# ScalarE's second exponentials ahead of its first cast, statistics of x1 behind the second maximum of slot 4, gates and bias scaled by GpSimd, in a gated attention block on one Trainium2 core

## The chip, the cores and the metric

One core of a Trainium2 chip. The metric is device time in microseconds, the median of several runs of the whole program. Engines: TensorE (PE; PEld for its weight loads), VectorE (DVE), ScalarE (ACT), GpSimd (POOL), SyncE (SP, which issues most DMAs). Each engine has a queue of its own that runs in the order of the program; queues wait for each other by semaphores.

## The reference, cut to what matters

```python
# x: 8 x 256 x 128, ctx: 8 x 512 x 128, 16 heads of 64, 8 experts of capacity 160
x = x + tanh(g_xattn) * xattn(layernorm(x), ctx)   # own layernorm, q, k, v, softmax, w_out, bias b_out, times tanh(gate)
x = x + tanh(g_ffn) * moe(layernorm(x))            # 8 experts, top 1, first come first served up to 160 tokens
```

For each of 8 batches `xattn` takes softmax(q k^T / 8) v over 512 context rows, for 16 heads and 256 queries; its output is projected, gets `b_out`, and is scaled by two tanh gates. What follows is called x1. Each row of x1 is normalised (a token), its router logits choose an expert, and the token's place among that expert's tokens decides whether it is kept.

## The kernel before, in words

**Slots.** The attention is cut into 8 batches of 8 slots; a slot is one pair of heads (`hp`, 0 to 7), numbered `j` = 8 x batch + `hp`, 64 in all. The order in every queue is written out by hand: each engine has a function `batch(b)` that goes over the slots and says what the engine does in each, with step constants (`PART_STEP`, `PROJECT_STEP`, ...) for the work that comes once a batch. A slot has two halves `qt` of 128 queries.

**What happens in a slot.** *TensorE* (lines 1429 to 1467): the scores of both halves, into psAB and psCD (`scores`, lines 1247 to 1272; the second half's wait for `exp_done` of the slot before), once-a-batch transposes, the transposes of finished outputs, the projections of k and q two slots ahead into psEF, in slot 1 and 3 the output projection of the batch before, a value projection into psX, and the value matmuls of the pair two slots back (`values`, lines 1274 to 1299), which read the transposed probabilities PT; 48 matmuls, half of them for each `qt`. *VectorE* (lines 1068 to 1117): the negated row maximum of half 0 and from it the bias NB (`row_max`, lines 910 to 917), the low part of the values (`v_lo`, line 907, waits for ScalarE's `v_hi` of the slot before), once-a-batch work, the maximum of half 1, the low part of k and q (`kq_lo`), and the normalising of the head outputs of two slots back. *ScalarE* (lines 787 to 806): the exponentials of half 0 (`exps`, line 757), the high part of k and q two slots ahead (`kq_hi`; not for pairs 0, 2 and 7 of a batch, which are kept whole), the cast of half 0's probabilities to 16 bits (`phi`, line 767), the exponentials of half 1, a copy of transposed outputs (`ot_copy`), the cast of half 1, and `v_hi` (line 724). *GpSimd* (lines 629 to 668): for each half, the low part of the probabilities that the cast left over (line 660), with some work of the batch ahead of, or behind, the two. *SyncE* (lines 487 to 500): for each half a DMA that transposes high and low part into PT (line 484), behind GpSimd's low part of that half.

Each matrix product is made of high and low parts, so the probabilities need both casts and the low parts before they are transposed.

**What the change touches.** `x_rstd`, `xn`, `token_rstd` and `token` of GpSimd normalise x for the next batch and tokens of the batch before. `token_moments` (lines 961 to 973) is VectorE's statistics of x1 for the batch before, in slot 3 behind `add_attention`, `kq_lo` and `normalise_heads`; GpSimd's `token_rstd` (lines 591 to 598) and first `token` stand at the head of slot 4, the second `token` at the head of slot 5, followed by `xt_lo` (line 558). In slot 2 of batch 0 VectorE multiplies two gates into `gscale` and scales `bo` by it (lines 1112 and 1115); `bo` is used by GpSimd from slot 7 on, `gscale` by VectorE from slot 1 of batch 1. The order on ScalarE now:

```python
exps(b, hp, 0)
kq_hi(*next_pair(b, hp, AHEAD))   # not for a whole pair
phi(b, hp, 0)
exps(b, hp, 1)
ot_copy(ot_pair(j))
phi(b, hp, 1)
v_hi(*v_group(b, hp))
```

Of the kernel before, what the change touches and what calls it, by code (L numbers as in the profile page):

```python
# [26 lines left out]
ALU = mybir.AluOpType  # L27
# [6 lines left out]
def gated_block(nc, x, ctx_1024, g_xattn, g_ffn, ln_gamma, ln_beta, w_q, w_kv, w_out, b_out, gate,  # L34
# [34 lines left out]
    with ExitStack() as ctx:  # L69
# [146 lines left out]
        bo_in = sem("bo_in")  # L216
# [149 lines left out]
        PART_STEP, CTX_STEP, PROJECT_STEP = 1, 2, 3  # L366
# [45 lines left out]
        BO_STEP, BIAS_STEP = 2, 7  # L412
# [115 lines left out]
        def _(pool):  # L528
# [100 lines left out]
            def batch(b):  # L629
                for j, hp in slots(b):  # L630
                    if hp == RSTD_STEP and not is_last(b):
                        x_rstd(b + 1)
# [8 lines left out]
                    if hp == PROJECT_STEP + 1 and not is_first(b):  # L641
                        token_rstd(b - 1)
                        token(b - 1, 0)
# [9 lines left out]
                    for qt in range(QT if j < LAST - 1 else LAST - j):  # L653
                        par = hp % 2

                        pool.wait_ge(phi_done[qt], j + 1)
                        if j >= 2:

                            pool.wait_ge(pt_in[qt][par], transposed_value(j - 2))
                        pool.tensor_tensor(PARTS[:, par, qt, 1], P32[:, par, qt], PARTS[:, par, qt, 0],  # L660
                                           ALU.subtract).then_inc(plo_done, 1)
                    if hp == LOGITS_STEP and not is_first(b):
                        mark_first(b - 1)
# [30 lines left out]
        def _(act):  # L694
# [92 lines left out]
            def batch(b):  # L787
                for j, hp in slots(b):
# [5 lines left out]
                    if j < LAST:  # L794
                        phi(b, hp, 0)
                    exps(b, hp, 1)
                    if ot_pair(j) >= 0:
                        ot_copy(ot_pair(j))
# [40 lines left out]
        def _(dve):  # L839
# [228 lines left out]
            def batch(b):  # L1068
                for j, hp in slots(b):
# [21 lines left out]
                    if hp == RANKS_STEP and b > 1:  # L1091
                        place(b - 2)
                    if j == LAST:
# [10 lines left out]
                    if hp == PROJECT_STEP and not is_first(b):  # L1104
                        token_moments(b - 1)
# [4 lines left out]
                    if is_first(b) and hp == BO_STEP:  # L1110
                        dve.wait_ge(tgate_done, 1)
                        dve.tensor_tensor(gscale[:], tgates[:, 0:1], tgates[:, 1:2], ALU.mult).then_inc(gscale_done, 1)
                        dve.wait_ge(gscale_done, 1)
                        dve.wait_ge(bo_in, 16)
                        dve.tensor_scalar(bo[:], bo[:], gscale[:, 0:1], None, ALU.mult).then_inc(bo_scaled, 1)
# [476 lines left out]
```

## Time and profile before

| | us |
|---|---|
| median of 3 runs | 463.63 (463.38 to 464.5) |
| the profiled execution's own time | 464.19 |
| its span, first to last instruction | 462.1 |
| one batch in the middle (slot 4 to slot 4) | 49.71 |
| TensorE busy | 432.6 (94%) |
| ScalarE busy | 381.7 (83%) |
| VectorE busy | 368.9 (80%) |
| GpSimd busy | 355.7 (77%) |

The profile is that of one execution. In its rows, `x4` is a count of instructions; a row of the timeline has the start and the length in us, engine, line, operation, out<-in by the program's names with shapes, and in brackets the idle time of the engine ahead of it and what ended that. Instructions of an engine overlap a little, so that from start to start they take less than their length. A row of the waits has who waited, the line, for whom, the total in us, how often, and the longest.

### The profile page before, as it was taken

What the parts mean: (1) busy time and instruction counts of PE and PEld (TensorE: products, weight loads), DVE (VectorE), ACT (ScalarE), POOL (GpSimd) and SP (SyncE); (2) the same over time, 40 slices, a digit from 0 to 9 for tenths busy, and PEclk for the clock granted to TensorE, in tenths of its full rate; (3) what the DMA queues carried; (4) which work ended last, traced back from release to release, by engine and by line L of the source; (5) the groups of instructions that cost most, each with busy time, mean ns of one, the idle gap of its engine ahead of it and who ended that gap; (6) DMA issues with size and microseconds to landing.
All of it is one profiled execution on the core that took longest, in us unless ns stands there. A gap on an engine that the chain in (4) does not pass through costs nothing.

```text
span 462.1 us, 13098 instructions
## 1 busy us (share of the span) xinstructions
PE 432.6 (94%) x5096; PEld 334.2 (72%) x5096; DVE 368.9 (80%) x803; ACT 381.7 (83%) x616; POOL 355.7 (77%) x270
## 2 busy tenths in 40 slices
PE   7887989999999999999999999999999999978993
PEld 6655757877777777776777777777777677757892
DVE  4788877799988898799879998899889887884622
ACT  5896979989988998899898998899889988981330
POOL 3686887788888897988888888898798887851325
PEclk9998999999999999999999999999999999989998
DMA  5998999999999999999999999999998999899111
GB/s 171 337 179 176 182 200 171 175 172 195 169 192 202 175 199 181 201 166 193 181 188 187 192 185 170 195 187 179 198 171 163 190 175 173 137 211 258 47 37 47
DMA packets 279964, 82.09 MB, mean 178 GB/s; under 512 B 264387, under 2 KB 276339, under 8 KB 279904
## 3 DMA queue, kind: packets, MB, share of 16 engines
q1 hardware_dynamic: 278528, 77.96, 94.8%
q0 software_dynamic: 1376, 3.30, 2.2%
q8 instruction: 41, 0.67, 0.6%
q14 instruction: 19, 0.16, 0.1%
HBM read 10.83 MB, written 5.14 MB: 35 GB/s over the span
## 4 chain that ended last, share of the span: by engine, by line
PE 65%; DVE 18%; ACT 8%; DMA 3%; issue 3%; POOL 2%; POOLq 0%; SPq 0%; ACTq 0%; DVEq 0%
DVE MXL L914 7%; PE psO L1295 5%; PE psO L1297 5%; PE psCD L1270 5%; PE psO L1296 5%; PE psAB L1263 4%; ACT P L757 4%; PE psCD L1263 4%; PE psAB L1270 3%; PE psEF L1191 3%; PE psEF L1193 3%; PE psEF L1192 3%; PE psEF L1310 3%; DVE HL L901 3%; PE psO L1356 3%
## 5 line engine op out<-in xcount | busy, mean ns | idle before, releaser
L660 POOL TENSOR_TENSOR PARTS<-P,PARTS 128x1024 f16<-128x1024 f32 x125 | 267.0, 2143 | 50.7 <-ACT PARTS L767 50.4
L767 ACT ACTIVATE PARTS<-P 128x1024 f16<-128x1024 f32 x126 | 135.2, 1073 | 0.8
L1295 PEld LDWEIGHTS psO<-VH,PT 128*128 128x128 f16 x1008 | 91.4, 98 | 21.2 <-issue 13.5
L1295 PE MATMUL psO<-VH,PT 128*128 128x65 f16 x1008 | 100.0, 196 | 3.0 <-DMA PT<-PARTS 1.6
L757 ACT ACTIVATE P<-psAB,NB 128x512 f32<-128x512 f32 x128 | 81.7, 698 | 25.1 <-DVE NB L917 24.9
L1296 PE MATMUL psO<-VL,PT 128*128 128x64 f16 x1008 | 99.3, 193 | 0.0
L1297 PE MATMUL psO<-VH,PT 128*128 128x65 f16 x1008 | 99.1, 194 | 0.0
L1296 PEld LDWEIGHTS psO<-VL,PT 128*128 128x128 f16 x1008 | 92.3, 99 | 0.1
L1297 PEld LDWEIGHTS psO<-VH,PT 128*128 128x128 f16 x1008 | 92.3, 98 | 0.0
L914 DVE TENSOR_REDUCE MXL<-psAB 128x2 f32<-128x1024 f32 x64 | 78.3, 1223 | 13.5 <-PE psAB L1263 6.7
L757 ACT ACTIVATE P<-psCD,NB 128x512 f32<-128x512 f32 x128 | 81.7, 701 | 1.9 <-DVE NB L917 1.0
L914 DVE TENSOR_REDUCE MXL<-psCD 128x2 f32<-128x1024 f32 x64 | 77.7, 1214 | 0.0
L907 DVE TENSOR_TENSOR VL<-psX,VH 128x512 f16<-128x512 f32 x63 | 43.2, 685 | 10.8 <-ACT VH L724 10.3
L1270 PE MATMUL psCD<-HL 64*128 64x512 f32 x252 | 37.9, 405 | 5.5 <-ACT P L757 5.5
L1270 PE MATMUL psAB<-HL 64*128 64x512 f32 x252 | 40.5, 426 | 0.8 <-ACT P L757 0.8
L901 DVE TENSOR_TENSOR HL<-psEF,HL 128x768 fp32r<-128x768 f32 x41 | 38.9, 950 | 2.8 <-ACT HL L719 1.7
L724 ACT ACTIVATE VH<-psX 128x512 f16<-128x512 f32 x63 | 38.6, 613 | 0.0
L1270 PEld LDWEIGHTS psCD<-HL 64*128 64x128 f32 x252 | 22.2, 184 | 17.2 <-ACT P L757 13.1
L1191 PE MATMUL psX<-w_hi,cT_hi 128*128 128x512 f32 x63 | 29.1, 462 | 5.8 <-DVE VL L907 5.6
L719 ACT ACTIVATE HL<-psEF 128x768 fp32r<-128x768 f32 x41 | 33.8, 824 | 0.9 <-PE psEF L1193 0.9
L746 ACT ACTIVATE OT<-psEF 128x256 f32<-128x256 f32 (+1 forms) x63 | 25.2, 400 | 10.7 <-PE psEF L1310 7.8
L1191 PE MATMUL psEF<-cT_hi,w_hi 128*128 128x512 f32 x63 | 30.1, 477 | 0.4 <-DVE cT_lo L889 0.4
(245 smaller groups left out, 858.9 us busy)
## 6 DMA issues: line engine op xcount, KB each, us to landing
ctx_raw<-in_ctx_dram SPq DMA_DIRECT2D x8, 256.0 KB, 4.1
w1s<-in_L_ffn_w_dram SPq DMA_DIRECT2D x8, 256.0 KB, 6.6
w2s<-in_L_ffn_w_dram SPq DMA_DIRECT2D x8, 256.0 KB, 4.6
PT<-PARTS SPq DMA_TRANSPOSE x126, 5.2
experts_table<-zeros POOLq DMA_DIRECT2D x2, 645.0 KB, 5.8
X<-in_x_dram SPq DMA_DIRECT2D x8, 128.0 KB, 3.4
wraw<-in_L_xattn_w_kv_dram SPq DMA_DIRECT2D x4, 256.0 KB, 4.9
out_dram<-row SPq DMA_DIRECT2D x8, 128.0 KB, 2.6
```

Of the source, the lines that this page charges most:

```text
L660: pool.tensor_tensor(PARTS[:, par, qt, 1], P32[:, par, qt], PARTS[:, par, qt, 0], ALU.subtract).then_inc(plo_done, 1)
L724: act.activation(VH[:, kt, 8 * half:8 * half + 8, 0:DH], bank[:].rearrange("p (h d) -> p h d", d=DH), ACT.Copy).then_inc(v_hi_done, 1)
L757: last = act.activation(P32[:, par, qt, SK * h:SK * h + SK], score_bank(qt)[:, SK * h:SK * h + SK], ACT.Exp, bias=NB[:, par, qt, h:h + 1])
L767: act.activation(PARTS[:, hp % 2, qt, 0], P32[:, hp % 2, qt], ACT.Copy).then_inc(phi_done[qt], 1)
L901: dve.tensor_tensor(hl[:, H_KLO:H_KLO + KQ], kq_bank(j)[:, 0:KQ], hl[:, H_KHI:H_KHI + KQ].bitcast(F32), ALU.subtract).then_inc(kq_done, 1)
L907: dve.tensor_tensor(VL[:, kt, 8 * half:8 * half + 8, :], bank[:].rearrange("p (h d) -> p h d", d=DH), VH[:, kt, 8 * half:8 * half + 8, 0:D ...
L914: dve.tensor_reduce(MXL[:, par, qt, :, 0], score_bank(qt)[:].rearrange("p (h n) -> p h n", h=2), AX.X, ALU.max, negate=True).then_inc(max_ ...
L1191: pe.matmul(dst, hi_l, hi_r, start=True, stop=False)
L1270: last = pe.matmul(score_bank(qt)[:, SK * h:SK * h + SK], hl[rows, q + P * qt:q + P * qt + P], hl[rows, k:k + SK], start=(q == H_QHI and k ...
L1295: pe.matmul(psO[:, g:g + DH + 1], phi, VH[:, kt, head, 0:DH + 1], start=first_, stop=False)
L1296: pe.matmul(psO[:, g:g + DH], phi, VL[:, kt, head, :], start=False, stop=False)
L1297: last = pe.matmul(psO[:, g:g + DH + 1], plo, VH[:, kt, head, 0:DH + 1], start=False, stop=last_)
```

## The change

On ScalarE, from slot 2 of batch 0 on, the second exponentials of every slot stand ahead of the first cast. VectorE's `token_moments` moves from the end of slot 3 to slot 4, behind the second maximum and ahead of `kq_lo`; GpSimd's `token_rstd` and the first `token` move from the head of slot 4 to between the two low parts of that slot. `gscale` and the scaled `bo` are computed by GpSimd at the head of slot 4 of batch 0 instead of by VectorE in slot 2; VectorE's waits for constants move to slot 7 of batch 0.

```diff
--- before.py
+++ after.py
@@ -363,7 +363,11 @@
 
             return {LAST: LAST, LAST - 1: LAST + 1}.get(j, j + 1)
 
-        PART_STEP, CTX_STEP, PROJECT_STEP = 1, 2, 3
+        def exps_together(j):
+
+            return j >= 2
+
+        PART_STEP, CTX_STEP, PROJECT_STEP, MOMENTS_STEP = 1, 2, 3, 4
         VALUES_BEHIND = 2
 
         def next_pair(b, hp, k):
@@ -409,7 +413,7 @@
         X_LOAD_STEP, WO_STEP = 1, 3
         STORE_STEP, TOKT_STEP, LOGITS_STEP, RANKS_STEP = 4, 5, 6, 0
 
-        BO_STEP, BIAS_STEP = 2, 7
+        BO_STEP, BIAS_STEP = 4, 7
 
         ROUTE = 14
         FULL = float(E * CAP - 1)
@@ -628,6 +632,12 @@
 
             def batch(b):
                 for j, hp in slots(b):
+                    if is_first(b) and hp == BO_STEP:
+                        pool.wait_ge(tgate_done, 1)
+                        pool.tensor_tensor(gscale[:], tgates[:, 0:1], tgates[:, 1:2], ALU.mult).then_inc(gscale_done, 1)
+                        pool.wait_ge(gscale_done, 1)
+                        pool.wait_ge(bo_in, 16)
+                        pool.tensor_scalar(bo[:], bo[:], gscale[:, 0:1], None, ALU.mult).then_inc(bo_scaled, 1)
                     if hp == RSTD_STEP and not is_last(b):
                         x_rstd(b + 1)
                     if hp == XN_STEP and not is_last(b):
@@ -638,9 +648,6 @@
                         i = b * QT
                         pool.tensor_tensor(X1[:, i:i + QT, :], X1[:, i:i + QT, :],
                                            bo[:].unsqueeze(1).to_broadcast([P, QT, D]), ALU.add).then_inc(x_biased, 1)
-                    if hp == PROJECT_STEP + 1 and not is_first(b):
-                        token_rstd(b - 1)
-                        token(b - 1, 0)
                     if hp == PROJECT_STEP + 2 and not is_first(b):
                         token(b - 1, 1)
                     if hp == X_STEP + 1 and not is_last(b):
@@ -659,6 +666,9 @@
                             pool.wait_ge(pt_in[qt][par], transposed_value(j - 2))
                         pool.tensor_tensor(PARTS[:, par, qt, 1], P32[:, par, qt], PARTS[:, par, qt, 0],
                                            ALU.subtract).then_inc(plo_done, 1)
+                        if qt == 0 and hp == MOMENTS_STEP and not is_first(b):
+                            token_rstd(b - 1)
+                            token(b - 1, 0)
                     if hp == LOGITS_STEP and not is_first(b):
                         mark_first(b - 1)
                     if is_first(b) and hp == LOGITS_STEP:
@@ -791,9 +801,11 @@
                     exps(b, hp, 0)
                     if not (is_last(b) and hp + AHEAD >= PAIRS):
                         kq_hi(*next_pair(b, hp, AHEAD))
-                    if j < LAST:
+                    if j < LAST and not exps_together(j):
                         phi(b, hp, 0)
                     exps(b, hp, 1)
+                    if j < LAST and exps_together(j):
+                        phi(b, hp, 0)
                     if ot_pair(j) >= 0:
                         ot_copy(ot_pair(j))
                     if j < LAST:
@@ -1090,6 +1102,8 @@
                         first_winner(b - 1)
                     if hp == RANKS_STEP and b > 1:
                         place(b - 2)
+                    if hp == MOMENTS_STEP and not is_first(b):
+                        token_moments(b - 1)
                     if j == LAST:
                         low_parts()
                         place(B - 2)
@@ -1101,18 +1115,12 @@
                         kq_lo(*next_pair(b, hp, AHEAD))
                     if VALUES_BEHIND <= j < LAST:
                         normalise_heads(*back(b, hp, VALUES_BEHIND))
-                    if hp == PROJECT_STEP and not is_first(b):
-                        token_moments(b - 1)
                     if j == 0:
                         x_moments(1)
                     if hp == X_STATS_STEP and b + 2 < B:
                         x_moments(b + 2)
-                    if is_first(b) and hp == BO_STEP:
-                        dve.wait_ge(tgate_done, 1)
-                        dve.tensor_tensor(gscale[:], tgates[:, 0:1], tgates[:, 1:2], ALU.mult).then_inc(gscale_done, 1)
+                    if is_first(b) and hp == X_STATS_STEP:
                         dve.wait_ge(gscale_done, 1)
-                        dve.wait_ge(bo_in, 16)
-                        dve.tensor_scalar(bo[:], bo[:], gscale[:, 0:1], None, ALU.mult).then_inc(bo_scaled, 1)
                         dve.wait_ge(ident_zero, 4)
                         dve.wait_ge(pool_consts, 5)
 
```

## Rows read from the trace of the kernel before

**Rows 1.** The page: busy time of the engines, share of the span.

```profile
PE 432.6 (94%) x5096; PEld 334.2 (72%) x5096; DVE 368.9 (80%) x803; ACT 381.7 (83%) x616; POOL 355.7 (77%) x270
```

**Rows 2.** Busy time in one batch: stretch, length, each engine's busy us.

```profile
291.25:340.96 49.71, 48.84 (x608) 37.03 (x605) 43.28 (x94) 45.65 (x74) 43.29 (x32) 1.00 1.09 183
```

**Rows 3.** The list of waits, whole run.

```profile
...
DVE VL L907 <- ACT VH L724: 10.3, 19, 1.3
...
PE psX L1191 <- DVE VL L907: 5.6, 8, 2.9
...
PE psCD L1270 <- ACT P L757: 5.5, 18, 1.4
...
PE psO L1295 <- DMA PT<-PARTS: 1.6, 2, 0.9
```

**Rows 4.** ScalarE's timeline, slots 4 to 6 of batch 6.

```profile
346.79 1.28 ACT L757 ACTIVATE P<-psCD,NB 128x512 f32<-128x512 f32 x2
...
351.26 1.06 ACT L767 ACTIVATE PARTS<-P 128x1024 f16<-128x1024 f32 x1
352.22 1.25 ACT L757 ACTIVATE P<-psCD,NB 128x512 f32<-128x512 f32 x2
353.36 0.38 ACT L746 ACTIVATE OT<-psEF 128x256 f32<-128x256 f32 x1
...
354.57 0.60 ACT L724 ACTIVATE VH<-psX 128x512 f16<-128x512 f32 x1
...
357.83 1.26 ACT L757 ACTIVATE P<-psCD,NB 128x512 f32<-128x512 f32 x2
```

**Rows 5.** VectorE's timeline, slots 3 to 6 of batch 6.

```profile
341.63 0.14 DVE L964 COPY mark<-gscale 128x1 f32<-128x1 f32 x1
...
342.54 1.22 DVE L914 TENSOR_REDUCE MXL<-psAB 128x2 f32<-128x1024 f32 x1
...
346.17 0.16 DVE L917 TENSOR_REDUCE NB<-MXL 128x2 f32<-128x4 f32 x1
...
350.41 0.41 DVE L885 COPY tT<-psO 128x256 f32<-128x256 f32 x1
...
355.24 0.68 DVE L907 TENSOR_TENSOR VL<-psX,VH 128x512 f16<-128x512 f32 x1
...
357.64 0.16 DVE L917 TENSOR_REDUCE NB<-MXL 128x2 f32<-128x4 f32 x1
```

**Rows 6.** TensorE's timeline: first scores of slots 4, 6 and 7 of batch 6.

```profile
340.96 0.96 PE L1270 MATMUL psAB<-HL 64*128 64x512 f32 x6
...
358.52 1.13 PE L1263 MATMUL psAB<-wraw 64*128 64x512 f32 x4
...
364.16 1.13 PE L1263 MATMUL psAB<-wraw 64*128 64x512 f32 x4
```

**Rows 7.** GpSimd's timeline, slots 4 and 5 of batch 6.

```profile
343.95 0.23 POOL L596 TENSOR_SCALAR vv<-mv 128x2 f32<-128x2 f32 x1
...
345.10 0.80 POOL L603 TENSOR_SCALAR row<-row,mv,rstd 128x128 f32<-128x128 f32 x1
346.99 2.15 POOL L660 TENSOR_TENSOR PARTS<-P,PARTS 128x1024 f16<-128x1024 f32 x1 [1.09 <-ACT PARTS L767]
349.36 2.15 POOL L660 TENSOR_TENSOR PARTS<-P,PARTS 128x1024 f16<-128x1024 f32 x1 [0.23 <-ACT PARTS L767]
...
352.94 4.26 POOL L660 TENSOR_TENSOR PARTS<-P,PARTS 128x1024 f16<-128x1024 f32 x2
```

**Rows 8.** VectorE's timeline, slots 2 and 3 of batch 0.

```profile
32.08 1.54 DVE L1112 TENSOR_TENSOR gscale<-tgates 128x1 f32<-128x1 f32 x1
33.65 2.26 DVE L1115 TENSOR_SCALAR bo<-bo,gscale 128x128 f32<-128x128 f32 x1
35.83 1.21 DVE L914 TENSOR_REDUCE MXL<-psAB 128x2 f32<-128x1024 f32 x1
```

**Rows 9.** Groups by line, slots 4 to 7 of batch 6.

```profile
L1295 PE MATMUL psO<-VH,PT 128*128 128x65 f16 x65 | 6.5, 195 | 0.0
```

**Rows 10.** SyncE's transposes (line 484), from 346 to 366 us.

```profile
DMA to landing us min/median/max: 4.5/5.4/6.4
```

## The prediction

> **What bounds the kernel now.** I read the page first: TensorE is busy for 94% of the span, ScalarE for 83% and its weight loads for 72% [rows 1]. An average says little, so next I cut one batch out of the steady middle: from the first scores of slot 4 of one batch to those of the next it lasts 49.71 us, of which TensorE works 48.84 and stands for 0.87 [rows 2]. So between these points only 0.87 us a batch can be won from waits, and any new wait of TensorE is paid in full. The list of waits names the few there are [rows 3]: the second scores (psCD) wait for ScalarE's second exponentials, the value projection (psX) for VectorE's low parts of the values, one time for 2.9 us, and only twice in the run the value matmuls wait for a transposed PARTS. The same list has VectorE's low value parts waiting 19 times for ScalarE's VH.
>
> That last wait belongs to a loop which the timelines show closed. In slot 5 of batch 6 ScalarE runs its first cast at 351.26 before its second exponentials at 352.22, then the other cast and VH to 355.17 [rows 4]. VectorE's VL starts 0.07 later, at 355.24, the second maximum is behind it on the same queue, its bias ends at 357.80 [rows 5], and the second exponentials of slot 6 start at 357.83 [rows 4]. Nothing in this ring idles: 5.61 us from second exponentials to second exponentials, 5.43 in the slot before (346.79 to 352.22). The first cast is not in it; it sits in the time in which ScalarE waits for the second bias. TensorE needs 23.20 for the four slots 4 to 7 (340.96 to 364.16 [rows 6]); without its waits there, 0.4 of psX in slot 4 (5.6 less the 2.9, over seven) and some 0.2 of psCD in slot 5 [rows 3], it would be 22.65, some 5.65 a slot. The ring and TensorE are almost level.
>
> **The change, part by part.** *Second exponentials ahead of the first cast.* No work is added on ScalarE; two things move. First, the cast enters the ring: behind the second exponentials it delays the second cast, so VH, so VL, so the next second maximum. It costs its pitch, 0.96 (351.26 to 352.22 [rows 4]). The ring becomes 6.39 and 6.57 for the steps into slots 5 and 6; for the steps into slots 7 and 0, where VectorE has next to nothing between VL and the maximum, I take 6.1 each (6.39 less some 0.3 for the token copy of 0.41 that stands there in slot 5 [rows 5]). Against TensorE's 5.65 this is the larger. Second, GpSimd's low part waits for that cast: it ends 2.2 behind the start of the second exponentials (their pitch 353.36 less 352.22, that is 1.14, and a cast of 1.06).
>
> *Statistics of x1.* Now they stand between slot 3's normalising and the first maximum of slot 4: 341.63 to 342.54, with the scores ready at about 341.95 [rows 5, 6]. Behind the second maximum they free 0.58, and the second exponentials of slot 4 no longer wait for the cast either: maximum at 1.0 after the slot's start, 3.79 from it to the second bias (342.54 to 346.33 [rows 5]), exponentials at 4.8 instead of 5.83. VectorE's low part of the keys moves back by 0.9 and has until the next slot; I cost it at nothing, and at most 0.5 a batch if that cover is short. What is late next is GpSimd: variance, square root and first token take 1.95 (343.95 to 345.90), now in an idle stretch ahead of slot 4's first low part; afterwards they stand between its two low parts, and slot 5's second token and x split (1.43, 351.51 to 352.94) follow at once [rows 7]. The waiting instruction there holds up the second low part, two transposes on SyncE behind it, and the value matmuls two slots later.
>
> *Gates and bias on GpSimd.* On VectorE the two instructions took 1.54 and 2.26 and held up slot 3's first maximum [rows 8]; the 2.9 us wait of psX behind it is TensorE's [rows 3]. On GpSimd by its nearest rows (0.23 for the short one, 0.80 for one of 128x128 [rows 7]) they take 1.1, in slot 4, where it waits for a cast; without that cover, 1.1 once. TensorE's wait shrinks to about 0.4, so the start gains 2.5; bounds 0 (all given back to late transposes) and 3.6 (nearly the 3.8 of the two instructions).
>
> **The sum over a batch**, times from the start of slot 4. *The ring:* second exponentials at 4.8, 11.2, 17.8, 23.9 in slots 4 to 7. TensorE's second scores of slot 0 need the end of the last (1.3 later, 25.2) and come 1.0 into the slot, so slot 0 starts at 24.2; the same wait a slot later makes it worth 24.4. *GpSimd:* first cast done at 7.0, low part to 9.25, tokens to 11.2, second low part to 13.35 (10.55 now), 1.43 and two low parts of slot 5 to 19.05 (16.24 now). The second halves of the value blocks, 0.8 long (6.5 us for the blocks of four slots [rows 9]), end where the next slot's scores begin [rows 6] and start at 16.75 in slot 6 and 22.4 in slot 7. With the median of 5.4 us from issue to landing [rows 10] the transposes now land at 15.95 and 21.64, 0.8 ahead. Both become 2.8 later: value matmuls wait in slot 6, slot 7 starts at 13.35+L+0.8 and slot 0 5.64 later, and the second gives slot 0 directly 19.05+L+0.8; both are about 19.85+L for a landing time L. The row has 4.5 at best and 6.4 at worst. The two of slot 4 are then 4.1 apart, nearly one after the other, so between 4.5 and 5.4 I take 5.0: slot 0 at 24.85. The remaining slots 0 to 3 take 49.71 less 23.20, less 0.3 for a gap that the earlier exponentials close: 26.2. A batch becomes 51.05, 1.35 more. Bounds: 50.6 (+0.9, L of 4.5, the ring alone) and 52.45 (+2.75, L of 6.4).
>
> The Trainium skill (DMA: Bandwidth & Descriptors, Latency and other measured facts) gives a DMA transpose 261 GB/s; for the 0.5 MB of one that is an estimate of 2.0 us and some 0.6 to the first byte, by which no transpose would be late and a batch would cost +0.9. The shortest landing here is 4.5 us, and the measurement decides.
>
> Six whole batches from slot 4 of batch 1 to that of batch 7: 6 x 1.35 = 8.1. The last batch's slots 4 to 7: 24.85 less 23.20, 1.65. The start: -2.5. Sum +7.25 on the profiled execution's own 464.19 (span 462.1 and 2.1 around it), 471.4; the median of the runs is 0.56 below that execution, so 470.9.
>
> **The rivals.** *Faster.* The ring has slack that I don't see, and late transposes are caught up: TensorE loses its 0.87 in six batches (5.2), 0.55 in the last, and 2.5 at the start: 455.4. It decides if the second bias comes under 5.65 after the last one although the cast is in front of VH. For it: ScalarE has 17% idle. Against: VL starts 0.07 after VH ends. The Trainium skill (Perfetto Trace Analysis, Identifying the Most-Contended Engine) looks for the engine of highest occupancy, TensorE judged by its weight loads; here that names ScalarE, 83% against 72%, and as no work is added to it, the change could not lose. The ring with no idle time speaks against it. 0.14.
>
> *Level.* Transposes are in time, and the ring is followed by slack slots that take most of it up: the four steps above are 25.2, and four more at 6.2 close it at 50.0, +0.3 a batch and 1.8 in all, which the start's 2.5 pays back: 462.9. Against it stands that slots 1 to 3 are bound by TensorE's own work, 20 of their 20.4 us, and can't make good what slots 5 to 0 lose. 0.12. That the change doesn't do what it says is no case: every queue runs in the order of the program.
>
> *Much slower.* Landings of 6.4 as a rule, because the late transposes of slot 5 meet those of slot 6: 6 x 2.75 + 3.05 - 2.5, 481. 0.06.
>
> **How the numbers follow.** The forecast has 0.68, with 466.5 (L of 4.5, start 3.6) to 477 (L near 5.9) as its own range. To leave out no more than 2 in 10 the range reaches down to the level case: 463 to 477. A measurement of this kernel can tell 0.3% from no change, 1.4 us. Faster 0.14, same 0.12, slower 0.74.
>
> **What would show it.** Right: ScalarE idle for about 0.9 ahead of the second exponentials in slots 5 to 7; VL still starting as VH ends, and 6.4 to 6.6 between second exponentials in slots 5 and 6; TensorE's waits for PT in slots 6 and 7 of every batch, one microsecond or so, where now there are two in the run; the wait of psX for VL gone, and the first maximum of slot 3 in batch 0 near 32.4 instead of 35.83; a batch of 50.6 to 51.5. Wrong: no wait for PT and a batch of 49 or less (the ring was not closed), or PT landing within 4 us, or a start that is not earlier.

## The result, and the profile after

The change makes the kernel **slower**: 479.0 us (478.74 to 481.11, 4 runs) against 463.94 (463.38 to 464.5, 4 runs) before it, a ratio of 1.0358 (95% interval 1.0328 to 1.0387). The forecast was 470.9, in a range of 463 to 477. The direction and, in the main, the mechanism were right; the size was not: the span grew by 14.3 us where the sum had 7.25.

First **where** the time went. The first scores of slot 4 in TensorE's timeline, read in each batch, cut the span (476.39 in the profiled execution of 478.86) into four stretches:

| stretch | before | after | difference | forecast |
|---|---|---|---|---|
| start to slot 4 of batch 1 | 92.38 | 90.48 | -1.90 | -2.5 |
| six batches, slot 4 to slot 4 | 297.85 | 310.17 | +12.32 | +8.1 |
| slot 4 to slot 7 of the last batch | 16.80 | 18.65 | +1.85 | +1.65 |
| slot 7 of the last batch to the end | 55.03 | 57.09 | +2.06 | 0 |
| span | 462.06 | 476.39 | +14.33 | +7.25 |

The page after, busy time and share of the span (to be held against [rows 1]), and the chain of work that ended last, by engine, of before and then of after:

```profile
PE 436.1 (92%) x5096; PEld 337.1 (71%) x5096; DVE 366.9 (77%) x801; ACT 381.0 (80%) x616; POOL 354.9 (75%) x272
```

```profile
PE 65%; DVE 18%; ACT 8%; DMA 3%; issue 3%; POOL 2%; POOLq 0%; SPq 0%; ACTq 0%; DVEq 0%
```

```profile
PE 42%; POOL 22%; DMA 11%; DVE 10%; issue 8%; ACT 3%; SPq 3%; POOLq 0%; DVEq 0%
```

No work was added; two small operations moved from VectorE to GpSimd, and the shares fell because the span grew. The chain shows it better: TensorE's part fell from 65% to 42%, and GpSimd and the DMA, 5% of it before, now have a third. Of that third the low parts are 19% of the span and the transposes behind them 9%.

One batch in the middle, to be held against [rows 2]:

```profile
296.23:348.41 52.18, 49.33 (x609) 37.39 (x606) 43.57 (x94) 45.57 (x74) 43.16 (x32) 1.00 1.00 168
```

It lasts 2.47 longer than the one of before, and TensorE stands for 2.85 of it, against 0.87. The list of waits after names what it stands for ([rows 3] are the same of before):

```profile
DVE VL L919 <- ACT VH L734: 21.8, 36, 1.3
...
PE psO L1303 <- DMA PT<-PARTS: 9.8, 16, 1.5
PE psX L1199 <- DVE VL L919: 8.4, 20, 0.7
```

The value matmuls wait for a transpose 16 times, not twice; the value projection (psX) waits for VectorE's VL 20 times, not 8; VL waits for ScalarE's VH 36 times, not 19. The waits of psCD fell from 5.5 to 1.8 us.

Now the loop of the prediction, on ScalarE's timeline in batch 6 (slot 4 starts at 348.41; compare [rows 4]):

```profile
353.23 1.26 ACT L767 ACTIVATE P<-psCD,NB 128x512 f32<-128x512 f32 x2 [0.40 <-DVE NB L929]
354.39 1.06 ACT L777 ACTIVATE PARTS<-P 128x1024 f16<-128x1024 f32 x1
...
359.56 1.27 ACT L767 ACTIVATE P<-psCD,NB 128x512 f32<-128x512 f32 x2 [0.95 <-DVE NB L929]
360.72 1.05 ACT L777 ACTIVATE PARTS<-P 128x1024 f16<-128x1024 f32 x1
...
362.87 0.60 ACT L734 ACTIVATE VH<-psX 128x512 f16<-128x512 f32 x1
...
366.11 1.26 ACT L767 ACTIVATE P<-psCD,NB 128x512 f32<-128x512 f32 x2 [1.48 <-DVE NB L929]
...
372.11 1.30 ACT L767 ACTIVATE P<-psCD,NB 128x512 f32<-128x512 f32 x2
```

The cast now stands behind the second exponentials, and ScalarE waits ahead of them, 0.95 and 1.48 us, for VectorE's bias. In slots 4 to 7 the second exponentials come 4.82, 11.15, 17.70 and 23.70 after the start of slot 4; forecast were 4.8, 11.2, 17.8 and 23.9. On VectorE's timeline VL still starts as VH ends (363.51, after 0.81 of waiting), with the maximum behind it:

```profile
363.51 0.69 DVE L919 TENSOR_TENSOR VL<-psX,VH 128x512 f16<-128x512 f32 x1 [0.81 <-ACT VH L734]
```

GpSimd's timeline of slots 4 and 5 (compare [rows 7]):

```profile
355.52 2.15 POOL L667 TENSOR_TENSOR PARTS<-P,PARTS 128x1024 f16<-128x1024 f32 x1 [2.56 <-ACT PARTS L777]
357.76 0.23 POOL L600 TENSOR_SCALAR vv<-mv 128x2 f32<-128x2 f32 x1
...
359.67 2.15 POOL L667 TENSOR_TENSOR PARTS<-P,PARTS 128x1024 f16<-128x1024 f32 x1
...
363.26 4.23 POOL L667 TENSOR_TENSOR PARTS<-P,PARTS 128x1024 f16<-128x1024 f32 x2
```

The low parts of slot 4 end 13.41 after its start (forecast 13.35), those of slot 5 at 19.08 (forecast 19.05). What TensorE makes of both, in its timeline of slots 5 to 7 and slot 0 of the next batch:

```profile
357.93 0.50 PE L1199 MATMUL psX<-w_hi,cT_hi 128*128 128x512 f32 x1 [0.63 <-DVE VL L919]
...
364.25 0.50 PE L1199 MATMUL psX<-w_hi,cT_hi 128*128 128x512 f32 x1 [0.27 <-DVE VL L919]
366.18 0.20 PE L1303 MATMUL psO<-VH,PT 128*128 128x65 f16 x1 [0.22 <-DMA PT<-PARTS]
...
370.81 0.50 PE L1199 MATMUL psX<-w_hi,cT_hi 128*128 128x512 f32 x1 [0.40 <-DVE VL L919]
...
373.61 0.20 PE L1303 MATMUL psO<-VH,PT 128*128 128x65 f16 x1 [1.11 <-DMA PT<-PARTS]
...
380.26 0.20 PE L1303 MATMUL psO<-VH,PT 128*128 128x65 f16 x1 [0.68 <-DMA PT<-PARTS]
```

Two kinds of waits alternate: the value projection cannot write psX before VL has read it (slots 5, 6, 7), and the second half of the values waits for its transpose (slots 6, 7, and slot 0 for the pair of slot 6). Over batches 2 to 6 the timelines give these means, in us:

| step into slot | from second exponentials to second exponentials: before, after (forecast) | TensorE's slot ahead of it: before, after (forecast) |
|---|---|---|
| 5 | 5.44, 6.33 (6.39) | 6.01, 5.43 |
| 6 | 5.61, 6.55 (6.57) | 5.92, 6.50 |
| 7 | 6.10, 6.00 (6.1) | 5.62, 6.79 |
| 0 | 5.26, 6.44 (6.1) | 5.61, 6.47 |
| slots 4 to 7 | 22.41, 25.32 (25.16) | 23.15, 25.19 (24.85) |
| slots 0 to 3 | | 26.58, 26.61 (26.2) |

The batches are not alike. Before, the six from slot 4 to slot 4 lasted 49.27 to 49.73; now they last 51.34, 51.17, 51.32, 51.92, 52.18 and 52.25.

### The profile page after: what moved, and what is told of

It reads as the page before. It is cut to its first block, busy times and chain, and to the rows that moved or that the text cites. A ratio compares the mean times of both kernels' runs of the same rounds, so it can differ in the third digit from the quotient of the medians.

```text
span 476.4 us, 13098 instructions
## 1 busy us (share of the span) xinstructions
PE 436.1 (92%) x5096; PEld 337.1 (71%) x5096; DVE 366.9 (77%) x801; ACT 381.0 (80%) x616; POOL 354.9 (75%) x272
## 4 chain that ended last, share of the span: by engine, by line
PE 42%; POOL 22%; DMA 11%; DVE 10%; issue 8%; ACT 3%; SPq 3%; POOLq 0%; DVEq 0%
POOL PARTS L667 19%; DMA PT<-PARTS 9%; DVE MXL L926 4%; PE psAB L1278 4%; PE psO L1303 3%; PE psO L1305 3%; PE psO L1304 3%; PE psO L1364 3%; PE psO L1403 3%; PE psAB L1271 2%; PE psCD L1278 2%; PE psCD L1271 2%; PE psEF L1537 2%; PE psEF L1199 2%; PE psEF L1200 2%
## 5 line engine op out<-in xcount | busy, mean ns | idle before, releaser
L1303 PE MATMUL psO<-VH,PT 128*128 128x65 f16 x1008 | 101.1, 195 | 12.3 <-DMA PT<-PARTS 9.8
L1304 PE MATMUL psO<-VL,PT 128*128 128x64 f16 x1008 | 100.4, 193 | 0.0
L1305 PE MATMUL psO<-VH,PT 128*128 128x65 f16 x1008 | 100.2, 194 | 0.0
L1278 PE MATMUL psCD<-HL 64*128 64x512 f32 x252 | 36.4, 393 | 1.8 <-ACT P L767 1.8
L937 DVE RECIPROCAL rden<-psO 128x4 f32<-128x4 f32 x64 | 11.6, 181 | 25.9 <-PE psO L1305 25.2
```

Source lines behind the costliest of these rows:

```text
L1278: last = pe.matmul(score_bank(qt)[:, SK * h:SK * h + SK], hl[rows, q + P * qt:q + P * qt + P], hl[rows, k:k + SK], start=(q == H_QHI and k ...
L1303: pe.matmul(psO[:, g:g + DH + 1], phi, VH[:, kt, head, 0:DH + 1], start=first_, stop=False)
L1304: pe.matmul(psO[:, g:g + DH], phi, VL[:, kt, head, :], start=False, stop=False)
L1305: last = pe.matmul(psO[:, g:g + DH + 1], plo, VH[:, kt, head, 0:DH + 1], start=False, stop=last_)
```

## The experiments

Theory 1: the order of the exponentials lengthens the loop VH, VL, second maximum, second exponentials, and the loop holds TensorE. Theory 2: the loss is late low parts and late transposes, whether the order or the tokens between the low parts make them late. The rivals beside them are that the other two parts of the change cost the time, or that the start does. All ratios are against the kernel before, on the same chip.

### One part of the change at a time

`a_exps` is before with the order of the exponentials alone:

```diff
-                    if j < LAST:
+                    if j < LAST and not exps_together(j):
                         phi(b, hp, 0)
                     exps(b, hp, 1)
+                    if j < LAST and exps_together(j):
+                        phi(b, hp, 0)
```

> The kernel before with the second exponentials ahead of the first cast and nothing else. Theory 1 (ring: the first cast now stands ahead of VH, and the ring over VL and the second maximum is longer than TensorE's slot): most of the loss is here, 1.2 to 1.6 us a batch and a slow last slot, ratio 1.020 to 1.030; 6.3 to 6.6 us between second exponentials in slots 5 and 6. Theory 2 (the tokens between GpSimd's low parts make the transposes late, the cast alone is covered): ratio 0.997 to 1.006.

`b_stats` is before with `token_moments` behind the second maximum of slot 4, and `token_rstd` and the first `token` between that slot's low parts:

```diff
-                    if hp == PROJECT_STEP + 1 and not is_first(b):
-                        token_rstd(b - 1)
-                        token(b - 1, 0)
...
+                        if qt == 0 and hp == PROJECT_STEP + 1 and not is_first(b):
+                            token_rstd(b - 1)
+                            token(b - 1, 0)
```

> The kernel before with the statistics of x1 behind the second maximum of slot 4 and the tokens between the two low parts, nothing else. Theory 1: the second low part of slot 4 ends only about 1.1 us later than now, the transposes have 0.8 to spare, TensorE loses its waits of psX and psCD in slots 4 and 5: ratio 0.992 to 1.003. Theory 2: 1.015 or more, with waits for PT in slots 6 and 7 of every batch.

`c_gates` is before with the gates and the bias on GpSimd, and `bc` has this and the statistics, without the order:

```diff
-                        dve.tensor_scalar(bo[:], bo[:], gscale[:, 0:1], None, ALU.mult).then_inc(bo_scaled, 1)
...
+                        pool.tensor_scalar(bo[:], bo[:], gscale[:, 0:1], None, ALU.mult).then_inc(bo_scaled, 1)
```

> The kernel before with the gates and the bias scaled by GpSimd, nothing else. Both theories: the 2.9 us wait of psX at 35 us goes, and with it the half clock behind it; slot 4 of batch 0 begins 4 us earlier, and if late transposes in slots 6 and 7 of that batch give back no more than half of that, ratio 0.990 to 0.996; if they give back all, 0.998 to 1.001.

> The changed kernel with the first cast back ahead of the second exponentials. Theory 1: the loss is gone, and the gains of the two other parts are left: ratio 0.985 to 0.998. Theory 2: still 1.010 or more above the kernel before, as the tokens still stand between the low parts.

Measured: `a_exps` 479.5, ratio 1.0353 (1.029 to 1.0416); `b_stats` 470.73, 1.0104 (1.0063 to 1.0145); `c_gates` 463.79, 0.9995 (0.9964 to 1.0027); `bc` 469.61, 1.0103 (1.0044 to 1.0163). TensorE's waits, of `a_exps` and then of `bc`:

```profile
PE psX L1197 <- DVE VL L913: 13.3, 27, 0.7
PE psO L1301 <- DMA PT<-PARTS: 5.6, 10, 1.5
```

```profile
PE psO L1297 <- DMA PT<-PARTS: 9.3, 13, 1.9
```

The order alone makes the whole loss, and more of it by VL than by late transposes. It lies above the range that theory 1 had for it (1.020 to 1.030). The statistics with the tokens alone make some 30% of it, and their waits are for transposes; `bc` falls where theory 2 had it, `b_stats` between the two theories. On top of the order they cost nothing that these intervals show. The runs of `b_stats` lie between 465.26 and 476.84, far apart for one kernel, and in one execution of `bc` a batch lasts from 49.47 to 52.80, with waits for PT in some batches and none in others. That fits transposes that are just late or just in time; no run separates it from another cause. The gates alone are worth nothing at the end: slot 4 of batch 0 starts 4.7 earlier (36.98 against 41.67), slot 4 of batch 1 only 2.7 earlier. Waits for PT (4.8 us, 6 times, against 1.6 before) take most of it, and the end, from slot 7 of the last batch on, is 1.1 longer (56.16 against 55.02).

### The change with one hold eased

`tok_head` has the tokens back ahead of slot 4's low parts. `vh_first` has VH ahead of both casts: the loop loses both casts, and the casts come 0.5 later. `vh_late` is `vh_first` with the tokens behind the low parts of slots 6 and 7.

```diff
+                    if v_group(b, hp) and exps_together(j):
+                        v_hi(*v_group(b, hp))
                     if j < LAST and exps_together(j):
                         phi(b, hp, 0)
...
-                    if v_group(b, hp):
+                    if v_group(b, hp) and not exps_together(j):
                         v_hi(*v_group(b, hp))
```

> The changed kernel with the tokens back ahead of slot 4's first low part (statistics still in slot 4). Theory 1 (the ring holds TensorE up, through the value projection that waits for VL): waits for PT in slots 6 and 7 shrink, the waits of psX for VL in slots 5 to 7 stay, 51.0 to 51.5 us a batch, ratio 1.022 to 1.030. Theory 2 (late transposes are all): without the 1.95 us between the low parts most of the loss goes, ratio 1.002 to 1.015.

> The changed kernel with the cast of the values (VH) ahead of both casts, directly behind the second exponentials: the ring no longer holds a cast, while the low parts come 0.5 us later still. Theory 1: the waits of psX for VL go, steps between second exponentials in slots 5 to 7 are no longer above 6 because of VL; what is left are waits for PT, 50.7 to 51.5 us a batch, ratio 1.012 to 1.028. Theory 2: worse than the changed kernel, ratio 1.036 or more.

> As vh_first, and the square root of the statistics at the head of slot 6, the two tokens behind the low parts of slots 6 and 7, so that no token stands ahead of a low part of slots 4 and 5. Theory 1: with ring and tokens out of the way the low parts are still 1.2 to 1.7 us later than before, against 0.8 to 1.5 to spare: ratio 0.995 to 1.010. Theory 2: the later casts alone make the transposes late, ratio 1.015 or more.

Measured: `tok_head` 476.73, 1.0285 (1.0245 to 1.0326); `vh_first` 489.23, 1.0578 (1.0508 to 1.0648); `vh_late` 479.77, 1.0332 (1.0273 to 1.0391). TensorE's waits of `tok_head`, then of `vh_first` (here a line of VectorE's stands too):

```profile
PE psX L1199 <- DVE VL L919: 11.1, 22, 0.7
PE psO L1303 <- DMA PT<-PARTS: 6.9, 8, 1.8
```

```profile
PE psO L1305 <- DMA PT<-PARTS: 22.0, 24, 2.5
...
DVE VL L921 <- ACT VH L734: 3.1, 3, 1.3
```

`tok_head` is where theory 1 had it. `vh_first` and `vh_late` are not: both lie where theory 2 had them, and there theory 1 by itself falls. With the loop cut in `vh_first` no wait of psX for VL is left on TensorE, and the kernel is slower than the change: with casts that are 0.5 later TensorE waits 22 us for transposes, and another 6.6 us in 19 waits ahead of its transposes of outputs, for which the profile names no cause. And with the tokens out of the way (`tok_head`) the value matmuls wait less for transposes (6.9 us against 9.8) and psX more for VL (11.1 against 8.4). Each time one hold is eased the other is there. So the two had to be made one at a time, on a kernel that has neither.

### Each hold alone

`late_tok` is that kernel: no change of order, statistics behind the second maximum of slot 4, gates on GpSimd, but the tokens of GpSimd behind the low parts of slots 6 and 7 (`token_rstd` at the head of slot 6), where nobody waits for what is behind them. In the last batch alone VectorE's statistics wait for the tokens; this holds for `vh_late` and every run below, too.

```diff
+                    if hp == 6 and not is_first(b):
+                        token_rstd(b - 1)
...
+                    if hp >= 6 and not is_first(b):
+                        token(b - 1, hp - 6)
```

> The kernel before with gates and bias on GpSimd and the statistics in slot 4, tokens moved as in vh_late, and the first cast ahead of the second exponentials as before. Both theories: ring as before, low parts of slot 5 0.8 us earlier than before, the start 4 us earlier with nothing given back: ratio 0.980 to 0.992. If the start is given back whatever the tokens do: 0.995 to 1.0.

Measured: 462.33, 0.9966 (0.9942 to 0.999), a batch of 49.36 on the mean of six, with psX waiting once (0.2 us) and four waits for PT, 4.1 us, all in batch 0. The range of both theories (0.980 to 0.992) was missed, the other reading met: the start is given back. Slot 4 of batch 0 starts 4.55 earlier than before, that of batch 1 only 0.76. And the end, from slot 7 of the last batch on, lasts 57.62 against 55.02.

`ring_only` adds a spare cast ahead of VH (its result is not used), so that only VH is late; `late_only` lets GpSimd wait for the second cast, so that only the low parts are:

```diff
+                    if hp >= 4 and not is_first(b) and j < LAST:
+                        act.activation(spare[:], P32[:, hp % 2, 1], ACT.Copy)
```

```diff
+                        if hp >= 4 and not is_first(b) and j < LAST - 1:
+                            pool.wait_ge(phi_done[1], j + 1)
```

> late_tok (0.9966, 49.4 us a batch) with one spare 128x1024 cast on ScalarE directly ahead of its VH in slots 4 to 7 of all batches but the first: VH comes later by about what the order of the change makes it, but no cast, low part or transpose does. The spare cast's result is not used. If the loop VH, VL, second maximum, second exponentials holds TensorE by itself: steps of the second exponentials into slots 5, 6, 7, 0 near 6.3, 6.55, 6.0 to 6.2, waits of TensorE for VL, few for PT, 51.4 to 51.6 us a batch, 1.020 to 1.030 against the kernel before. If late transposes are all of the loss: as late_tok, 0.995 to 1.003.

> late_tok with GpSimd's first low part in slots 4 to 7 of all batches but the first held until the second cast is through: the low parts and the transposes behind them come about as late as in the change, and ScalarE's order is that of the kernel before. If late transposes are a second, separate hold: waits of TensorE for PT, +0.85 to 1.3 us a batch over late_tok, 1.005 to 1.018 against the kernel before. If they are all of the loss: 1.020 or more. If they cost nothing alone: as late_tok, 0.995 to 1.000.

Measured: `ring_only` 483.73, 1.0449 (1.0393 to 1.0506); `late_only` 480.54, 1.0342 (1.0284 to 1.0399). TensorE's waits, of the first and of the second:

```profile
PE psX L1197 <- DVE VL L915: 17.8, 25, 1.1
...
PE psO L1301 <- DMA PT<-PARTS: 3.6, 5, 1.0
```

```profile
PE psO L1300 <- DMA PT<-PARTS: 22.3, 22, 2.4
...
PE psX L1196 <- DVE VL L914: 0.2, 1, 0.2
```

The two holds are clean, 25 waits for VL in the one and 22 for PT in the other, and both cost more than theory 1 had it, `late_only` as much as where late transposes are all of the loss: 3.54 and 3.03 us a batch over `late_tok` (means of six batches, 52.90 and 52.39), against 2.34 for the change. So each of the two makes a loss of this size without the other, and in the change they do not add. But the size of `ring_only` is not the loop's alone: the spare cast is also work on ScalarE. From 374.07 to 379.86 in its timeline, slot 7 of batch 6, ScalarE has no idle time at all, and VectorE's bias is ready 1.0 earlier (378.87), so there ScalarE's own queue sets the step (6.95, in the change 6.00). Its four steps sum to 26.33, those of the change to 25.32; less these 1.01, some 2.5 a batch remain, an estimate for the loop as the change has it.

To have a later VH without added work, `vh_next` puts VH behind both first exponentials of the next slot, `vh_mid` between them. `late_ot` lets GpSimd wait for the copy of transposed outputs, half as long as in `late_only`:

```diff
                     exps(b, hp, 0)
+                    if j > 0 and held(j - 1) and v_group(*divmod(j - 1, PAIRS)):
+                        v_hi(*v_group(*divmod(j - 1, PAIRS)))
...
-                    if v_group(b, hp):
+                    if v_group(b, hp) and not held(j):
                         v_hi(*v_group(b, hp))
```

```diff
+                        if qt == 0 and hp >= 4 and not is_first(b) and j < LAST - 1:
+                            pool.wait_ge(ot_done, ot_pair(j) + 1)
```

> late_tok (49.4 us a batch) with the VH of slots 4 to 7 (all batches but the first) behind both first exponentials of the next slot instead of ahead of them: 1.15 us later by their pitch, no work added on ScalarE and no cast later. If the loop through VL holds TensorE by itself: steps of the second exponentials into slots 5, 6, 7 near 6.75, waits of TensorE for VL, hardly any for PT, 52.3 to 53.3 us a batch, 1.038 to 1.050 against the kernel before. If the loss of ring_only was ScalarE's added work: 49.4 to 50.0 a batch, 0.996 to 1.005.

> The same with VH between the two first exponentials of the next slot: 0.58 us later. If the loop through VL holds TensorE by itself: steps near 6.2, 50.9 to 51.5 us a batch, 1.018 to 1.028 against the kernel before, about half of what vh_next loses. If the loss of ring_only was ScalarE's added work: as late_tok, 0.996 to 1.003.

> late_tok with GpSimd's first low part in slots 4 to 7 (all batches but the first) held until the copy of transposed outputs, which stands between the second exponentials and the second cast: the first low part starts 1.5 us behind the second exponentials, against 0.1 in late_tok and 2.5 in late_only, and the second low part ends 1.15 us later than in late_tok, against 2.15. If the price of late transposes grows with the delay: about half of late_only's 2.7 us a batch, 50.6 to 51.0, 1.012 to 1.020. If it begins only past a threshold: 49.4 to 50.2, 0.996 to 1.008.

Measured: `vh_next` 515.51, 1.1139 (1.1101 to 1.1176); `vh_mid` 491.7, 1.0625 (1.0586 to 1.0663); `late_ot` 474.28, 1.0263 (1.0224 to 1.0302). In `vh_mid` psX waits 27.2 us (25 times) and PT 3.4 (3 times); in `vh_next` it is 41.0 and 3.9. So a later VH with no work added stops TensorE through VL; added load on ScalarE is not needed for it. But both cost far more than expected, and VectorE's timeline of `vh_next` shows that I had built another loop:

```profile
390.22 0.69 DVE L917 TENSOR_TENSOR VL<-psX,VH 128x512 f16<-128x512 f32 x1 [1.82 <-ACT VH L732]
...
397.54 0.69 DVE L917 TENSOR_TENSOR VL<-psX,VH 128x512 f16<-128x512 f32 x1 [1.82 <-ACT VH L732]
...
405.06 0.69 DVE L917 TENSOR_TENSOR VL<-psX,VH 128x512 f16<-128x512 f32 x1 [1.82 <-ACT VH L732]
```

VL comes every 7.3 to 7.5 us, and VectorE waits 1.82 each time from the first bias to VH. Behind the first exponentials VH waits for the first maximum, that for TensorE's next scores, those stand behind the value projection, and that waits for VL: TensorE's own work has come into the loop. These two runs therefore give no price for the 0.96 us of the change. `late_ot` is clearer: 1.59 us a batch on the mean of six (49.74 to 53.60) in its profiled execution, the quickest of its four at 470.74, and above the expectation in the ratio. The price grows with the delay: half the delay has half the price of `late_only` by the profiled executions (1.59 of 3.03 us a batch) and two thirds by the medians (12 of 18 us over `late_tok`). Two points show no threshold, but cannot rule out a small one.

### A version that is faster than both

`late_tok` loses 4 us in batch 0 to waits for PT, 2.9 of it in two (1.41 and 1.52) beside the load of `wo`. `wo_early` issues that load at the start; `wo_early2` has also the order of the change, in slot 2 of each batch alone.

```diff
             for piece in range(E):
                 expert_piece(piece)
+            sp.dma_start(wo[:], w_out.rearrange("(c p) n -> p c n", p=P)).then_inc(wo_in, 16)
...
-                    if is_first(b) and hp == WO_STEP:
-                        sp.dma_start(wo[:], w_out.rearrange("(c p) n -> p c n", p=P)).then_inc(wo_in, 16)
```

> late_tok with the load of wo issued at the start, behind the pieces of w1, not beside the first transposes of batch 0. If the two waits of 1.4 and 1.5 us in batch 0 of late_tok are that load's: they are gone, 458.5 to 460 us, 0.988 to 0.993. If the start then waits for something else: as late_tok, 0.996.

> wo_early with the second exponentials ahead of the first cast in slot 2 of each batch alone, where no new values are projected: the psCD wait of slot 3 (0.32 us a batch) goes and no loop through VL is touched: 456.5 to 459 us, 0.984 to 0.991. If the order costs something in itself, whatever the slot: slower than wo_early by 1 us or more.

Measured: `wo_early` 461.03, 0.993 (0.990 to 0.996); `wo_early2` 462.02, 0.9957 (0.993 to 0.9984). Both expectations were too good. The two waits are gone, and TensorE's timeline of `wo_early` has another, one slot earlier:

```profile
50.32 0.24 PE L1297 MATMUL psO<-VH,PT 128*128 128x65 f16 x1 [2.37 <-DMA PT<-PARTS]
```

In `wo_early2` the waits of psCD fall from 5.4 to 2.9 us, as meant, and those for PT rise from 3.1 to 5.9. One of them, 1.23 in slot 4 of batch 0, is for the pair of slot 2, whose low parts the order makes later; the others are for pairs of other slots, and what makes them is not shown. Between the two the intervals overlap. `wo_early` is the best of the study, 0.7% below the kernel before and, by the two ratios, some 4% below the change (0.993 against 1.0358).

## Why the prediction was right and wrong

In short: the loop came as forecast and the transposes nearly so. **The step that failed** is the sum over a batch, 1.35 more in the forecast and 2.05 measured, and in it first the 26.2 of slots 0 to 3; the tail, put at nothing without a reason, added 2.06.

**The loop: right.** The steps into slots 5, 6 and 7 were 6.33, 6.55 and 6.00 against 6.39, 6.57 and 6.1, and the cause was the one given: a cast moved behind the exponentials stands in front of VH, and VL starts as VH ends. In slot 7 too the loop is closed: VectorE's bias ends at 372.08, 0.03 ahead of the second exponentials, although ScalarE has other work up to then. The step into slot 0 was 6.19 in batches 2 to 4; in 5 and 6 it was 6.61 and 7.02, because TensorE started slot 0 late.

**The loop's grip on TensorE: incomplete.** I let the loop reach TensorE at one place, the second scores of slot 0, and wrote that the wait of psX for VL would be gone. It is gone once, in batch 0. In every later batch the same buffer, psX, ties TensorE to the loop: 20 waits, 0.63 in slot 5, 0.27 in slot 6 and 0.40 in slot 7 of batch 6. The runs with a later VH alone show this link. That it changed the sum little in slots 4 to 7 I put down to the other hold, which was nearly level; no run shows it for the change itself.

**The transposes: right in form, sizes a little short.** GpSimd's times were right to 0.06, and slot 0 starts at 19.08 plus the landing plus 0.83, as written. In batches 1 to 4 slots 4 to 7 lasted 24.77 to 24.97, as forecast (24.85), and in 5 and 6 25.41 and 26.03; the mean of batches 2 to 6 is 25.19. The difference is the landing of slot 5's second transpose, counted from the end of its low part: 5.0 in the sum, 4.75 to 5.02 in batches 1 to 4, 5.45 and 6.07 in 5 and 6. There SyncE took 2.95 and 2.96 us to issue the transpose ahead of it (1.75 to 2.03 in batches 2 to 4) and so issued it 0.93 behind the low part. Why that issue took longer stays open.

**Slots 0 to 3: a credit that was spent.** I took 0.3 off for the psCD gap in slot 3. That slot did get 0.23 shorter, but slot 0 got 0.24 longer in the mean, because in batches 5 to 7 it waits for the transpose of slot 6's pair as well (0.68, 0.50 and 0.68). I had followed the late low parts through slots 4 and 5 and not into slot 6. Of all terms this is the one that failed most: 26.61 instead of 26.2. With the 0.34 of slots 4 to 7 it makes, within 0.05, the 2.05 a batch (12.32 over six) where the sum had 1.35, hence 4.2 of the 7.1 us that were missing.

**The tail: costed at nothing, 2.06.** TensorE's timeline in the change, and stretches of it (length, each engine's busy us, then the granted clock):

```profile
416.10 0.19 PE L1303 MATMUL psO<-VH,PT 128*128 128x65 f16 x1 [1.56 <-issue]
...
417.87 0.24 PE L1303 MATMUL psO<-VH,PT 128*128 128x65 f16 x1 [0.89 <-DMA PT<-PARTS]
...
419.30 2.08 PE L1271 MATMUL psAB<-wraw 64*128 64x512 f32 x4
421.17 1.92 PE L1271 MATMUL psCD<-wraw 64*128 64x512 f32 x4
...
440.56 0.69 PE L1505 MATMUL psAB<-ident,PARTS 128*128 128x128 f32 x4 [1.15 <-DMA PARTS<-experts_table]
...
442.65 1.92 PE L1419 MATMUL psCD<-ident 128*128 128x128 f32 x8
```

```profile
414.00:416.00 2.00, 0.54 (x5) 0.30 (x4) 1.16 (x4) 2.00 (x4) 2.00 (x2) 1.00 0.67 131
416.00:418.00 2.00, 1.01 (x27) 0.93 (x28) 1.88 (x7) 0.52 (x2) 2.00 (x2) 0.79 1.02 211
418.00:420.00 2.00, 2.00 (x26) 1.71 (x26) 0.56 (x2) 2.00 (x3) 0.48 (x1) 0.50 1.12 214
...
442.00:444.00 2.00, 2.00 (x11) 2.00 (x11) 1.61 (x9) 1.32 (x4) 0.00 (x0) 0.50 0.00 0
```

The same of the kernel before:

```profile
427.41 0.66 PE L1497 MATMUL psAB<-ident,PARTS 128*128 128x128 f32 x4
...
428.96 1.06 PE L1411 MATMUL psCD<-ident 128*128 128x128 f32 x8
```

```profile
414.00:416.00 2.00, 2.00 (x24) 1.94 (x23) 1.22 (x1) 1.13 (x2) 1.21 (x2) 0.50 1.11 208
```

In the change two waits close together, with TensorE busy for 0.54 and 1.01 of two stretches of 2 us, are followed by 6 us at a granted clock of 0.50 (418 to 424), the lower of its levels (1.2 GHz). The profile puts the first wait down to nothing; VL of the slot ends 0.10 ahead of its end. The scores of slot 7 take 2.08 and 1.92 at that clock, where four such matmuls took 1.13 in [rows 6] (whose three rows are the first scores of slots 4 and 7 and of the next batch's slot 0), and they end 1.28 later behind the slot's start than before. But TensorE makes that good, as it had a stretch at 0.50 before as well, only later (414 to 416, in slot 7): its first matmul with `wo` comes 9.74 behind the start of slot 7, against 10.12.

What stays late is another chain. VectorE's last low part stands behind the maximum of those scores, so SyncE issues the last transpose 7.19 behind the start of slot 7, against 6.04, and the load of the experts' table, which stands behind it on SyncE, lands 21.22 behind that start, against 20.34. TensorE waits 1.15 for it and goes on 0.88 later than before; and this wait is again followed by a stretch at 0.50 (442 to 444), in which eight matmuls take 1.92 in place of 1.06. From the experts' first product on everything is 2.06 later. So 0.88 is the late load, and the other 1.18 the second stretch at the lower clock.

This is read from the rows; no run was made for it. And the tail is not tied to the order alone: over the traces of all kernels here it lasts 55.0 to 58.9, and 57.6 in `late_tok`, whose scores of slot 7 are not slow.

**The start: -1.90 for -2.5.** The gates do take 0.19 and 0.61 on GpSimd (1.1 were allowed), the first maximum of slot 3 comes at 32.86 (32.4 forecast), and slot 4 of batch 0 starts 4.4 earlier. That is more than the lost wait of 2.9: before, TensorE was granted 0.50 from 38 to 40 us behind that wait, and now 1.00. Then, up to slot 4 of batch 1, 2.5 is given back, with waits of 1.48 and 0.94 for PT and of 0.34 and 0.66 for VL in batch 0; the lower bound of that term allowed for it.

**The rivals.** *Faster* needed slack in the loop; there was none. The Trainium skill (Perfetto Trace Analysis, Identifying the Most-Contended Engine) takes the engine of highest occupancy as the most contended one. Here occupancy gave no sign of the loss: ScalarE's share fell from 83 to 80% while an order of its queue cost 3.5%; what counted was its place in a loop. *Level* needed slots 1 to 3 to make good what 5 to 0 lose; they didn't. *Much slower* was nearest in time (481), but by landings of 6.4 as a rule, and they were 5.0 in the median (5.2 before): the nearness is chance. The range ended at 477 because it had landings near 5.9 as its only way up, and nothing for slot 0's wait or the tail.

## What to carry to other kernels

When a loop over several engines has no idle time, ask at which buffers the busiest engine touches it, every one of them; here the value bank was one and the score bank the other, and the one I left out was in the list of waits already. Work that is merely reordered has a price at each consumer of what became later, so follow a late product until it is used, also into the next batch; two holds that are nearly level don't add, and easing one of them shows only the other. A run that is to make one thing late should add no work to the engine and bring no new engine into the loop.

## What the runs showed of the hardware

Two short waits of TensorE, less than 3 us in all, were followed by 6 us at half its clock, in which a slot's scores ended 1.28 later than before; after one wait of 1.15 the clock fell again, and the stretch cost 1.18. Before, VectorE's product of 128x1 and its scaling of 128x128 took 1.54 and 2.26 us and ended, at 33.62 and 35.91, about as two low parts of GpSimd did (4.38 for both, from 31.45 to 35.83); GpSimd does them in 0.19 and 0.61. GpSimd's timeline of before, to be held against [rows 8], and then that of the change:

```profile
31.45 4.38 POOL L660 TENSOR_TENSOR PARTS<-P,PARTS 128x1024 f16<-128x1024 f32 x2 [1.63 <-ACT PARTS L767]
```

```profile
42.73 0.19 POOL L637 TENSOR_TENSOR gscale<-tgates 128x1 f32<-128x1 f32 x1
43.03 0.61 POOL L640 TENSOR_SCALAR bo<-bo,gscale 128x128 f32<-128x128 f32 x1
```

The Trainium skill (Advanced Engine Details and Errata, VectorE Performance Modes) says that GpSimd shares VectorE's second port to SBUF, so that instructions of GpSimd and those of VectorE that use both ports block each other. That fits, but no row tells whether these two used both ports, and no run here separates it from another cause. A transpose landed 4.3 us after its issue at best, 5.0 in the median and 7.5 at worst in the change (92 to 390 us; the trace tells the landing of 70 of 94), and 4.3, 5.2 and 7.8 before. So the transposes were late because they were issued late, not because they took longer.
